# A two-part graph and attention kernel on one Trainium2 core: its attention stage written in units of four heads in place of two

## The reference

```python
h = _sln(hidden, w, ...)                       # gamma * layer_norm + beta
qkv = (h @ Wqkv.T + bqkv).reshape(B, N, 16, 32, 3)
energy = einsum('bhqd,bhkd->bhqk', q, k)
att = softmax(energy, axis=-1) / D ** 0.5
out = einsum('bhqk,bhkd->bhqd', att, v)  ->  @ Wp.T + bp
h1 = out + hidden
return _sln(h1, w, ...) + h1
```

## Time and profile before

| | |
|---|---|
| runs shown, median (lowest to highest) | 1630.13 us (1624.61 to 1631.23) |
| the profiled execution's own time | 1630.67 us |
| its span | 1628.9 us |
| busy: PE, DVE, ACT, POOL | 1490.8, 977.9, 722.8, 395.5 us |
| mean granted clock of TensorE | 0.964 |
| prologue, graph, attention stage | 0 to 114.6, 114.6 to 583.5, 583.5 to 1628.9 us |

### The profile page before, as it was taken

The page is one execution under the profiler, slowest core; times in us unless marked ns, Lnnn a source line. Parts: engine busy times, 40 slices in busy tenths (PEclk is TensorE's granted clock), DMA queues, the critical chain, the costliest instruction groups (busy, mean ns, idle before and its releaser), DMA issues. The chain is left out here.

```text
span 1628.9 us, 21550 instructions
## 1 busy us (share of the span) xinstructions
PE 1490.8 (92%) x7204; PEld 896.1 (55%) x7204; DVE 977.9 (60%) x1454; ACT 722.8 (44%) x1250; POOL 395.5 (24%) x266
## 2 busy tenths in 40 slices
PE   6979899999999628999999999999999999999993
PEld 4636666666666425555655654655654655554632
DVE  2533676667666623556666666666666666666675
ACT  0231342334233242565465465465465465465471
POOL 1013443334332141011042041032042042041032
PEclk9999899999999858999999999999999999999997
DMA  9453233223331243223124124124124124123121
GB/s 301 167 204 79 83 134 140 105 109 139 133 136 53 81 161 104 49 63 118 42 67 141 45 63 136 43 65 144 43 64 143 41 66 141 46 62 107 46 54 66
DMA packets 97176, 162.17 MB, mean 100 GB/s; under 512 B 39104, under 2 KB 47616, under 8 KB 90928
## 3 DMA queue, kind: packets, MB, share of 16 engines
q1 hardware_dynamic: 95920, 160.44, 31.9%
q10 hardware_dynamic: 1152, 0.41, 0.1%
HBM read 72.67 MB, written 37.78 MB: 68 GB/s over the span
## 5 line engine op out<-in xcount | busy, mean ns | idle before, releaser
L1171 DVE TENSOR_REDUCE mx<-a_bank 128x1 f32<-128x512 f32 x512 | 340.0, 687 | 226.0 <-PE a_bank L1356 223.6
L1071 ACT ACTIVATE pt<-a_bank 128x512 f32<-128x512 f32 x512 | 277.2, 595 | 148.8 <-PE a_bank L1381 145.9
L1395 PE MATMUL a_bank<-pt,v 128*32 128x512 f32 x1024 | 272.5, 608 | 0.0
L1397 PE MATMUL a_bank<-pt,ones 128*32 128x512 f32 x1024 | 272.5, 608 | 0.0
L1356 PE MATMUL a_bank<-sk_stack,sq_stack 96*128 96x512 f32 x512 | 207.6, 446 | 5.2 <-DVE mx L1171 2.0
L1356 PEld LDWEIGHTS a_bank<-sk_stack,sq_stack 96*128 96x128 f32 x512 | 88.5, 189 | 187.8 <-DVE mx L1171 135.1
L1381 PE MATMUL a_bank<-sq_stack,sk_stack 98*128 98x512 f32 x512 | 169.6, 408 | 2.8 <-ACT pt L1071 1.4
L742 PE MATMUL g_bank<-m,sf 128*128 128x320 f32 x512 | 155.1, 446 | 1.9 <-issue 1.9
L1062 ACT ACTIVATE sq_stack<-a_bank 2x512 fp32r<-2x512 f32 x128 | 69.0, 583 | 146.9 <-PE a_bank L1365 146.7
L48 PE MATMUL a_bank<-hh,wqkh 128*128 128x512 f32 x256 | 107.2, 419 | 25.4 <-POOL hl L971 24.6
L1381 PEld LDWEIGHTS a_bank<-sq_stack,sk_stack 98*128 98x128 f32 x512 | 96.6, 191 | 43.9 <-ACT pt L1071 15.1
(11 more groups left out here) (166 smaller groups left out, 2652.1 us busy)
## 6 DMA issues: line engine op xcount, KB each, us to landing
sq_stack<-qh SPq DMA_DIRECT2D x256, 64.0 KB, 2.0
sk_stack<-kh SPq DMA_DIRECT2D x256, 64.0 KB, 2.0
m_rows<-mout SPq DMA_DIRECT2D x8, 1280.0 KB, 5.0
m<-m_rows SPq DMA_DIRECT2D x8, 1280.0 KB, 5.7
xraw<-in_x_t SPq DMA_DIRECT2D x8, 1024.0 KB, 7.7
xn<-in_x SPq DMA_DIRECT2D x8, 1024.0 KB, 5.2
h_rows<-xn SPq DMA_DIRECT2D x8, 1024.0 KB, 4.0
t_rows<-hout SPq DMA_DIRECT2D x8, 1024.0 KB, 3.9
```

The lines of the kernel that those rows point to most:

```text
L1071: nc.scalar.activation(pt[:, i, k, :], bank[:, k, :], ACT.Exp).then_inc(s["exp_done"], 1)
L1171: nc.vector.reduce_max(mx[:, p % 2, n, k:k + 1], bank[:, 2 + i % 2, :], AX).then_inc(s["emax_done"], 1)
L1395: nc.tensor.matmul(bank[a:a + DH, 4 + p % 2, :], v[:, bpar, i, (2 * p + k) * DH:(2 * p + k + 1) * DH], w, start=i == 0, stop=i == NT - 1)
L1397: last = nc.tensor.matmul(bank[r:r + DH, 4 + p % 2, :], ones32[:, :], w, start=i == 0, stop=i == NT - 1)
```

## The change

Graph stage: bp is added to the residual rows by GpSimd (`add_bp`), and h_rows then holds x + bp; the transposed layer norm is written in two halves (high by ScalarE's second scaling, low by GpSimd's `lo_rows`), t_rows doubles. bp is loaded before GpSimd starts. Attention stage: units of four heads with 16 slots; a slot is a shifted score of this unit, a score of the next, and three matmuls of some projection. `weighted` runs four heads side by side with v only; the key sums are added up by GpSimd over the four key tiles (`key_sum`, into acc) and reduced by four matmuls (`denominators`). The shift rows are transposed in one instruction per half (16x128), copied by ScalarE and put into the stack by a DMA of SP (`shift_rows`). The reciprocals are taken from PSUM in four pieces of 128 columns. Statistics, normalisation and results go tile by tile. The split of h and `h + bp` are gone from this stage.

```diff
             def store_h(b, four):
-                sp.wait_ge(s["h_done"], four)
+                sp.wait_ge(s["hb_done"], four)
                 sp.dma_start(d["h_rows"][ds(b, 1)].rearrange("o p t f -> (o p) t f"), xn[:, :, :]).then_inc(s["h_stored"], 16)
             def store_t(b, four):
-                sp.wait_ge(s["lnt_done"], four)
-                sp.dma_start(d["t_rows"][ds(b, 1)].rearrange("o p c n -> (o p) c n"), hout[:, :, :]).then_inc(s["t_stored"], 16)
+                sp.wait_ge(s["hl_done"], four)
+                for k, src in enumerate((houth, houtl)):
+                    sp.dma_start(d["t_rows"][ds(b, 1), k].rearrange("o p c n -> (o p) c n"), src[:, :, :].bitcast(F32)
...
                 load_v(b)
                 store_h(b - 1, 4 * b)
                 sp.wait_ge(s["h_stored"], 16 * b)
-                sp.wait_ge(s["ln_done"], 4 * b)
                 load_x(b)
                 if not last:
                     sp.wait_ge(s["sc_ready"], 4 * b + 4)
...
             load_adj(0)
             load_m(0)
+            sp.dma_start(bp[:, :], d["bp"].partition_broadcast(P)).then_inc(s["bp_in"], 16)
...
+            def add_bp(b):
+                for i in range(NT):
+                    pool.wait_ge(s["ln_done"], 4 * b + i + 1)
+                    nc.gpsimd.tensor_tensor(xn[:, i, :], xn[:, i, :], bp[:, :], ALU.add).then_inc(s["hb_done"], 1)
+            def lo_rows(b):
+                for f in range(FC):
+                    pool.wait_ge(s["lnt_done"], 4 * b + f + 1)
+                    nc.gpsimd.tensor_tensor(houtl[:, f, :], hout[:, f, :], houth[:, f, :].bitcast(F32),
+                                            ALU.subtract).then_inc(s["hl_done"], 1)
...
             def step(b, par, last):
                 if not last:
                     front(b + 1)
+                if not (isinstance(b, int) and b == 1):
+                    lo_rows(b - 2)
                 softmax(b, True)
+                add_bp(b - 1)
                 if not last:
                     label_products(b + 1)
+            pool.wait_ge(s["bp_in"], 16)
...
+            lo_rows(B - 2)
             back(B - 1)
+            add_bp(B - 1)
+            lo_rows(B - 1)
...
             def scale_ln(b, f):
                 if f == 0:
                     act.wait_ge(s["gb_in"], 16 * 2 * FC)
-                    act.wait_ge(s["t_stored"], 16 * b)
+                    act.wait_ge(s["t_stored"], 32 * b)
                 act.wait_ge(s["lnt_ready"], 4 * b + f + 1)
                 nc.scalar.activation(hout[:, f, :], bank[:, 2 + f, :], ACT.Identity,
+                                     bias=bcol[:, f, ds(b, 1)], scale=gcol[:, f, ds(b, 1)])
+                nc.scalar.activation(houth[:, f, :], bank[:, 2 + f, :], ACT.Identity,
                                      bias=bcol[:, f, ds(b, 1)], scale=gcol[:, f, ds(b, 1)]).then_inc(s["lnt_done"], 1)
...
+            def key_sum(b, c, half, step):
+                G, two = 4 * b + c, slice(2 * half, 2 * half + 2)
+                done = 6 * G + 3 * half
+                if step == 0:
+                    pool.wait_ge(s["exp_done"], SLOTS * G + 8 * half + 4)
+                    if half == 0 and not start(b, c):
+                        pool.wait_ge(s["den_ready"], G)
+                    nc.gpsimd.tensor_tensor(acc[:, two, :], pt[:, 0, two, :], pt[:, 1, two, :],
+                                            ALU.add).then_inc(s["sum_done"], 1)
+                else:
+                    pool.wait_ge(s["exp_done"], SLOTS * G + 8 * half + 2 * step + 4)
+                    pool.wait_ge(s["sum_done"], done + step)
+                    nc.gpsimd.tensor_tensor(acc[:, two, :], acc[:, two, :], pt[:, step + 1, two, :],
+                                            ALU.add).then_inc(s["sum_done"], 1)
...
+                    if not start(b, c):
+                        key_sum(*(ahead(b, c, -1) if c else (b - 1, 3)), 1, 2)
+                    if later and c in (1, 2):
+                        rsqrt(b - 1, 2 * c - 2)
+                    if later and c in (2, 3):
+                        result(b - 1, 2 * c - 3)
+                    key_sum(b, c, 0, 0)
+                    if later and c in (1, 2):
+                        result(b - 1, 2 * c - 2)
+                    key_sum(b, c, 0, 1)
+                    key_sum(b, c, 0, 2)
+                    key_sum(b, c, 1, 0)
+                    if later and c in (1, 2):
+                        rsqrt(b - 1, 2 * c - 1)
+                    key_sum(b, c, 1, 1)
...
+            def load_t(b):
+                if not first(b):
                     act.wait_ge(s["k_ready"], 4 * b)
-                nc.scalar.activation(hh[:, f, :], traw[:, f, :], ACT.Copy).then_inc(s["hh_done"], 1)
+                    act.wait_ge(s["v_ready"], 4 * b)
+                for part in range(2):
+                    two = slice(2 * part, 2 * part + 2)
+                    for k, dst in enumerate((hh, hl)):
+                        act.dma_start(dst[:, two, :].bitcast(F32),
+                                      d["t_rows"][ds(b, 1), k, :, two, :].rearrange("o p c n -> (o p) c n")
+                                      ).then_inc(t_in[part], 16)
...
+            def shift_copy(b, c, half):
+                n = 2 * (4 * b + c) + half
+                act.wait_ge(s["sh_ready"], n + 1)
+                if not (isinstance(b, int) and n == 0):
+                    act.wait_ge(s["shrow_in"], 16 * n)
+                nc.scalar.activation(sht[:, :], bank[0:4 * NT, XB, 0:P], ACT.Copy).then_inc(s["sht_done"], 1)
...
+            def exp(b, c, slot):
+                G = 4 * b + c
+                half, i, k = slot // 8, slot % 8 // 2, slot % 2
+                if k == 0 and not start(b, c):
+                    if i == 0:
+                        act.wait_ge(s["pv_done"], 2 * G - 1)
+                        act.wait_ge(s["sum_done"], 6 * G + 3 * half - 5)
+                    if i == 2:
+                        act.wait_ge(s["pv_done"], 2 * G)
+                        act.wait_ge(s["sum_done"], 6 * G + 3 * half - 4)
+                    if i == 3:
+                        act.wait_ge(s["sum_done"], 6 * G + 3 * half - 3)
+                act.wait_ge(s["et_ready"], SLOTS * G + slot + 1)
+                nc.scalar.activation(pt[:, i, 2 * half + k, :], bank[:, k, :], ACT.Exp).then_inc(s["exp_done"], 1)
...
+            def reciprocals(b, c, piece):
+                G, col = 4 * b + c, slice(piece * P, (piece + 1) * P)
+                if piece == 0:
+                    dve.wait_ge(s["den_ready"], G + 1)
+                    if not (isinstance(b, int) and G < 2):
+                        dve.wait_ge(s["ol_done"], G - 1)
+                nc.vector.reciprocal(rden[:, c % 2, col], bank[:, XB, col]).then_inc(s["rden_done"], 1)
...
             def quotients(b, c):
...
-                nc.vector.scalar_tensor_tensor(o[:, :], oraw[:, :], float(D) ** -0.5, rden[:, :],
+                G = 4 * b + c
+                dve.wait_ge(s["pv_done"], 2 * G + 2)
+                dve.wait_ge(s["rden_done"], 4 * G + 4)
+                nc.vector.scalar_tensor_tensor(rden[:, c % 2, :], bank[:, OB, :], float(D) ** -0.5, rden[:, c % 2, :],
...
+                            lo_part(*ahead(b, c, 2), 0)
+                        if 6 <= slot < 10 and former:
+                            reciprocals(*former, slot - 6)
+                        if slot == 7 and (c < 3 or more):
+                            shift_parts(*ahead(b, c, 1), 0)
+                        if slot == 9 and (c < 2 or more):
+                            lo_part(*ahead(b, c, 2), 1)
+                        if slot == 10 and former:
+                            quotients(*former)
+                        if slot == 13:
...
+            def shift_t(b, c, half):
+                n = 2 * (4 * b + c) + half
+                pe.wait_ge(s["sh_lo"], n + 1)
+                if not (isinstance(b, int) and n == 0):
+                    pe.wait_ge(s["sht_done"], n)
+                if half == 0 and not (isinstance(b, int) and n <= 2):
+                    pe.wait_ge(s["rden_done"], 4 * (4 * b + c - 1))
+                nc.tensor.transpose(bank[0:4 * NT, XB, 0:P], parts[:, :, :, :].rearrange("p o k n -> p (o k n)").bitcast(F32),
+                                    t["ident"][:, :].bitcast(F32)).then_inc(s["sh_ready"], 1)
+            def weighted(b, vpar, c, part):
+                G = 4 * b + c
+                pe.wait_ge(s["exp_done"], SLOTS * G + 12 + 4 * part)
+                if part == 0 and not start(b, c):
+                    pe.wait_ge(s["o_done"], G)
+                if c == 0:
+                    pe.wait_ge(s["v_done"], 4 * b + 2 + 2 * part)
+                for i in (2 * part, 2 * part + 1):
+                    for j in range(HC):
+                        last = nc.tensor.matmul(bank[DH * j:DH * j + DH, OB, :],
+                                                v[:, vpar, i, (HC * c + j) * DH:(HC * c + j + 1) * DH], pt[:, i, j, :],
```

(38 more changed lines are left out.)

849 lines of the change are left out of this document (401 added, 448 removed).

## The result

The changed kernel takes 1679.3 us in the median of 4 runs (1676.1 to 1683.9) against 1629.4 for the one before: a ratio of 1.031, 95% interval 1.028 to 1.035. The profiled execution has a span of 1677.2 us against 1628.9, 48.3 more. The windows by stage answer to the earlier trace rows (the graph stage ends where the attention stage issues its first instruction, at 693.4); columns are the same: us, busy time of PE, PEld, DVE, ACT and POOL, granted clock, DMA share, GB/s.

A forecast was written before the change was run, and what follows sets the result against it. TensorE was taken to bound the attention stage, while it stands at some point of every graph step. From 1630.7 us, 103 saved in attention and 116 added in the graph stage gave 1644, range 1590 to 1695.

The forecast's parts named there:

- TensorE's own saving: Attention units: weighted sums 3.1 us and shift rows 1.3 us less per unit, leaving 24.1 us of own work.
- Rival 4: Attention stage: matmuls with four different moving operands do not run side by side; 160 us more, 1800; chance 0.03.
- The graph stage: Late xraw and low clock 90 us, last step 11, end 8, start 7; together +116, bounds 43 and 148.
- Rival 2: Graph stage: the xraw load is not late, 12 us per step go; 60 us less, about 1584; chance 0.13.
- lies beside it: Graph steps: label sum 5.1 us later on GpSimd, counted as hidden beside the 18 us of xraw delay and low clock.
- A steady batch at 110 us: Attention stage: units of 27.1, 27.1, 26.1 and 29.4 us; 12.5 less per batch, 75 in six; ends 102 and 118.
- about +3 us in one of four: Attention units 1 to 3: GpSimd's result tiles make key sums late for the denominators or exponentials; about +3 us in one of four.
- The plain unit at 27.1: Attention unit: 24.1 us of own work, 1.2 for VectorE's burst, 1.0 and 0.8 for shift instructions behind key sums.
- Batch 0 at 97 us: First attention batch, with no older results on GpSimd: from 115.2 us to 97, 18 less.
- the last batch and tail: End of the attention stage, 139.4 us before: half the shift and projection work, so 11 us less.
- Rival 1: Attention stage: key sums meet VectorE at harmless moments, a batch takes 102 us; 60 less, 1584; chance 0.22.
- Rival 3: Attention stage: GpSimd or VectorE become the bound, a batch takes 118 us; 60 more, 1704; chance 0.12.

The follow-up runs named there:

- e3: Changed kernel with the shift split into high and low parts after its transposition, read from PSUM, key sums whole; 1628.7 us, ratio 0.999.
- e1: Changed kernel with the load of the next xraw issued before the store of h on SP; 1638.5 us, ratio 1.005.
- e2: Changed kernel with GpSimd's key sums over 16 of 512 columns, the rest left out, all waits kept; 1598.4 us, ratio 0.981.
- e4: Changed kernel with each reciprocal over 8 of its 128 columns, the rest of the division left out; 1623.9 us, ratio 0.995.
- e8: Changed kernel with each key sum of 128x1024 made of two instructions of 128x512; 1651.4 us, ratio 1.012.
- e12: e7 with bp's addition, store of h and load of x moved to the next step, key sums over 16 columns; 1530.2 us, ratio 0.939.
- e7: e1 and e3 together, bp added after the label products and awaited later, three output lo parts per batch moved to slots 4 and 5; 1550.4 us, ratio 0.950.
- e11: e7 with bp's addition, store of h and load of x moved to the next step, key sums split as in e8; 1544.9 us, ratio 0.948.

## Why the prediction was wrong

Its direction, its mechanisms and its range (1590 to 1695) held; its size did not: 14 us slower were forecast, 50 came. The step that failed is the saving of 103 us in the attention stage: 61.6 came. A steady batch was put 3.4 us too short, and batch 0 was priced as if it had no key sums. By its steps:

- **TensorE's own saving: right.** Half of a unit's weighted sums (two steps of the forecast, sixteen records) takes 1.92 us and the denominators (one step, eight records) 1.07, as against 1.9 and 1.0. Where nothing stands in the way a unit takes 24.7 us (e3), 24.1 were worked out. Rival 4 is out: four different moving operands run side by side.

```profile
862.41 1.92 PE L1436 MATMUL a_bank<-pt,v 128*32 128x512 f32 x16
...
867.97 1.07 PE L1447 MATMUL a_bank<-acc,ones 128*32 128x512 f32 x8
```

- **The graph stage: right in size, +109.9 against +116.** Rival 2 is out. The late xraw was forecast at 13 us of ScalarE's idle time and shows 13.22; five steps are 84 us longer from store to store, 90 were forecast; GpSimd's first work starts at 124.07 in place of 115.56, 8.5 us against 7. The sentence that the late label sum "lies beside it" was the weak one: by itself (e1) it still costs about 5 us and a low clock per step, so that taking the load's delay away gives back 41 us and not 62.
- **A steady batch at 110 us: too short by 3.4, so 20 us in six.** The term that failed most is "about +3 us in one of four", which I put down to late key sums. The long unit is 31.5 us in the mean against 29.4, and its row shows what makes it long: two output lo parts, whose waits the sum did not price though the earlier trace rows had shown one at 1.82, and a shift instruction, all in a row behind key sums. The other three take 81.9 together against 80.3. e2 splits the miss: with small key sums a batch takes 103.4 us, where the forecast without its terms for them is 4 x 25.3 = 101.2. So about 2.2 us of the 3.4 are other work, in the two units in which VectorE also has statistics, results and lo parts (27.0 and 26.1 us there), and 1.2 are key sums, 10.0 against 8.8. That the burst of VectorE and the collisions are the causes is shown by e2, e3 and e4.
- **The plain unit at 27.1: met, but partly by luck.** The sum was 24.1 of own work, 1.2 for VectorE's burst and 1.8 for the shift instructions. The runs show 24.7 (e3), 0.3 (e2 against e3) and 2.2 (the changed kernel against e2), again 27.2. The 1.2 also rests on a wrong addition: the instructions listed for the burst come to 9.4 us with a quotient at 0.68, not 8.3, and the order printed above the prediction has one lo part there, not two.
- **Batch 0 at 97 us: wrong by 14, the last batch and tail by 7.** I took batch 0 without GpSimd's old results as if it were without key sums too (97 is four times the bottom of 24.1); it has all of them (57 us of GpSimd's work in 111), its eight shift instructions take 11.3 us, and its units, from denominators to denominators, are 28.0, 30.1 and 27.1 us long. With small key sums (e2) they are 26.4, 26.5 and 24.9, which accounts for 7.5 of the 14; the rest stays open, with a mean clock of 0.92 there. From the denominators at 1548.17 to the end the changed kernel takes 129.0 us, e2 116.2: the key sums cost more there than the 7 us that were missed.
- **Sum.** 20 + 14 + 7 is 41 us too little cost in the attention stage, 6 too much in the graph stage: 35, the distance from +13 to +48 in spans.
- **Rival 1** (a batch of 102) is out at 113.4. **Rival 3** (a batch of 118 with VectorE or GpSimd as the bound) is half true: in the six batches TensorE stands 52.1 us for VectorE's maxima, more than for anything else. The Trainium skill (SBUF — State Buffer, section "Who interferes with whom") says that of VectorE and GpSimd the one that issues first has the shared port pair for its whole instruction. e8 agrees for VectorE as the second: with GpSimd's instruction at 1.28 us in place of 2.39, the longest wait leaves 1.27 us for 2.30.

What stays open: why the shift rows come late once per batch from e3 on, half of batch 0's miss, and what the second scaling costs in a graph step that doesn't wait for x.

## What to carry to other kernels

An addition that moves to an idle engine is not free when it stops a busy one's instructions on SBUF, as GpSimd's did here: look at which operands of the busy engine's instructions are in SBUF, and move them to PSUM (e3: 51 us for a reordered split) or shorten the other engine's instructions (e8: 28 us) before giving up the saving. When a wait is inserted in front of a DMA, read what stands behind it on that queue; and when two delays lie beside each other, price both, since the shorter one is what is left after the longer is cured. And after such a move look for the next wait: here it was a small DMA (13 us in six batches, e3 to e12). With the shift split in PSUM and xraw loaded first, the same rewrite that was 3.1% slower is 5% faster than the kernel before (e7 to e11).
